# Local attention blocks: probabilities turned whole and placed by copies, the sum of the rotated keys on another engine

## The reference, cut to what matters

```python
def look(t):
    p = jnp.pad(t, ((0, 0), (0, 0), (1, 0), (0, 0), (0, 0)))
    return jnp.concatenate([p[:, :, :nw], p[:, :, 1:]], axis=3)
...
q = l2norm(q) * qs
k = l2norm(k) * ksc
...
k = k * cos * inv + rotate_half(k) * sin * inv
...
sim = jnp.einsum('bhwie,bhwje->bhwij', bq, bk2) * QK_SCALE
sim = jnp.where(mask, -jnp.finfo(sim.dtype).max, sim)
attn = jax.nn.softmax(sim, -1)
out = jnp.einsum('bhwij,bhwje->bhwie', attn, bv2)
...
for i in range(DEPTH):
    x = attn_layer(shift_tokens(x), Wqkv[i], q_scale[i], k_scale[i], Wo[i]) + x
    x = ffn_layer(shift_tokens(x), ln_g[i], ln_b[i], W1[i], b1[i], W2[i], b2[i]) + x
return x
```

## Time and profile before

| | |
|---|---|
| median of 3 runs | 3162.67 us |
| lowest and highest | 3152.88, 3163.48 us |
| the profiled execution's own time | 3146.83 us |
| its span, first to last instruction | 3144.8 us |
| mean granted TensorE clock | 0.954 of full speed |
| busy, share of the span | TensorE 88%, VectorE 78%, ScalarE 67%, GpSimd 43% |
| copies of `v_edge`, 128 KB each | 96 |

### The profile page before, as it was taken

How to read it: one execution, slowest core, us unless ns; L and a number is a source line. 1 busy time by engine, 2 the same in 40 slices (tenths; PEclk the granted TensorE clock), 3 DMA queues, 4 the chain that set the end, 5 groups by cost and what they waited for, 6 DMA issues and landing times. The chain is left out here.

```text
span 3144.8 us, 72108 instructions
## 1 busy us (share of the span) xinstructions
PE 2774.6 (88%) x27244; PEld 1692.0 (54%) x27244; DVE 2442.2 (78%) x3071; ACT 2104.3 (67%) x3079; POOL 1351.6 (43%) x1209
## 2 busy tenths in 40 slices
PE   5799999997678989888889898989999999789997
PEld 3122222223546565656566666656665656478885
DVE  3899999992379797979798888888888979455554
ACT  2488888885158787878788787878787878311111
POOL 1000000000078685867586758676766767200000
PEclk7799999998589999999999999999999999889998
DMA  3011111100010001000100010001000000000001
GB/s 131 27 29 28 28 29 29 29 24 8 8 57 9 6 9 43 7 8 9 42 9 6 17 34 9 8 15 36 8 7 14 15 7 9 12 18 0 0 0 34
DMA packets 56465, 64.35 MB, mean 20 GB/s; under 512 B 24742, under 2 KB 38964, under 8 KB 55348
## 3 DMA queue, kind: packets, MB, share of 16 engines
q1 hardware_dynamic: 55380, 60.58, 7.0%
q10 hardware_dynamic: 864, 0.79, 0.1%
HBM read 36.69 MB, written 7.34 MB: 14 GB/s over the span
## 5 line engine op out<-in xcount | busy, mean ns | idle before, releaser
L886 DVE TENSOR_REDUCE a_minus_max<-a_ps_max 128x1 f32<-128x1024 f32 x512 | 596.8, 1218 | 57.6 <-PE a_ps_max L811 52.3
L794 ACT ACTIVATE a_expT<-a_ps_scoresT 128x512 f32<-128x512 f32 (+1 forms) x683 | 528.8, 808 | 78.2 <-PE a_ps_scoresT L829 67.4
L1178 POOL TENSOR_TENSOR b_turned_q<-b_rot_q,b_turned_q 128x1024 f32<-128x1024 f32 x96 | 226.8, 2362 | 270.2 <-DVE b_turned_q L1549 257.3
L844 PE MATMUL a_ps_out<-a_expT,v_aug 128*32 128x256 f32 x4096 | 327.9, 392 | 5.4 <-ACT a_outT L781 4.8
L1620 DVE STREAM_TRANSPOSE b_probsT<-b_probs 32x512 f32<-32x512 f32 x384 | 269.4, 702 | 11.9 <-POOL b_probs L1219 0.3
L765 POOL CAST a_max_hi<-a_minus_max 128x16 bf16<-128x16 f32 x32 | 6.3, 198 | 631.1 <-DVE a_minus_max L886 631.1
L1287 ACT ACTIVATE b_kT<-b_psD 64x512 f32<-64x512 f32 x384 | 226.1, 589 | 58.6 <-PE b_psD L1374 53.5
L829 PE MATMUL a_ps_scoresT<-a_q_op,a_k_op 26*128 26x512 bf16 x1024 | 247.2, 385 | 13.1 <-ACT a_expT L794 4.4
L1225 POOL TENSOR_TENSOR b_turned_k<-b_rot_k,b_turned_k 128x512 f32<-128x512 f32 x192 | 243.9, 1270 | 0.2 <-DVE b_turned_k L1549 0.2
L1185 POOL TENSOR_TENSOR b_rot_q<-b_turned_q,b_inv_norm 128x1024 f32<-128x1024 f32 x96 | 182.8, 1904 | 137.7 <-issue 137.7
L1219 POOL TENSOR_TENSOR b_probs<-b_probs,b_inv_sum 128x512 f32<-128x512 f32 x192 | 197.3, 1049 | 99.1 <-DVE b_inv_sum L1593 99.1
(11 more groups left out here) (295 smaller groups left out, 6019.4 us busy)
## 6 DMA issues: line engine op xcount, KB each, us to landing
b_v_edge<-b_v SPq DMA_DIRECT2D x96, 128.0 KB
b_w_qkv<-L_ffn_Wqkv SPq DMA_DIRECT2D x6, 1536.0 KB
a_q_op<-terms_q SPq DMA_DIRECT2D x128, 48.0 KB
a_k_op<-terms_k SPq DMA_DIRECT2D x128, 48.0 KB
joined<-a_outT SPq DMA_DIRECT2D x256, 16.0 KB
b_w_o<-L_ffn_Wo SPq DMA_DIRECT2D x6, 512.0 KB
a_q_op<-a_max_rows SPq DMA_DIRECT2D x128, 4.0 KB
b_w<-L_ffn_W SPq DMA_DIRECT2D x6, 341.0 KB
```

The lines of the kernel that those rows point to most:

```text
L794: act.activation(expT[:, to:to + 512 * size], ps_scoresT[:, at:at + 512 * size], ACT.Exp, scale=SCALE_A).then_inc(exp_ready, 1)
L844: last_mm = pe.matmul(ps_out[lo:lo + 32, 256 * part:256 * part + 256], v_aug[:, b * T8 + kt, head, :], expT[:, at:at + 256], start=(kt == ...
L886: dve.tensor_reduce(minus_max[p % 2][:, side, 0, qt:qt + 1], ps_max[u % 2][:], AX.X, ALU.max, negate=True).then_inc(max_taken, 1)
L1178: pool.tensor_tensor(turned[:], rot[:], turned[:], ALU.add).then_inc(added, 1)
```

## The change

The own half of the probabilities is transposed in one instruction over all 128 partitions into a new buffer `packed_own`, as the look-back half was into `packed`. `probsT` is laid out as partition, window of the query, head, 32 queries, so that every block of 32 partitions and one window is one run of 512 numbers. From the two buffers eight copies issued by SP, each of 32 partitions by 512 numbers, place the blocks: four out of `packed` (one to `edgeT`, three to `probsT`) and four out of `packed_own`. The copies of ScalarE (L1272, L1273) and GpSimd (L1201) go, with `ones`. The value matmuls read their 128 columns as four pieces of 32.

The sum of the two key products is formed by VectorE, in one instruction over all 16 heads right behind the second product; GpSimd's two additions go, and its two multiplications wait for that sum.

The next layer's 1.5 MB of projection weights are loaded in six parts of 256 KB, one in each step of the loop of a layer's first half, behind the eight copies.

VectorE waits for the previous tile's copies to have left `packed` and `packed_own` before it writes them again; TensorE waits for all eight in front of the value matmuls.

```diff
-        probsT = sb("probsT", [P, HEADS_B, P])
+        packed_own = sb("packed_own", [P, HEADS_B, W])
+        probsT = sb("probsT", [P, P // W, HEADS_B, W])
         edgeT = sb("edgeT", [P, HEADS_B, W])
-        ones = sb("ones", [P, HEADS_B])
...
+            def load_qkv_part(l, slot, part):
+                at = slot * 3 * INNER + part * 512
+                sp.dma_start(w_qkv[:, ds(at, 512)], wts["Wqkv"][ds(l, 1), :, ds(part * 512, 512)].rearrange("o p n -> p (o n)")).then_inc(w_qkv_in, 16)
...
             def step(l, b, s, par, lags, ahead=None):
+                T = l * TILES + b * T8 + s
                 if 0 in lags:
-                    T = l * TILES + b * T8 + s
                     sp.wait_ge(v_held, 2 * T + 2)
                     sp.dma_start(v_edge[par][P - W:P, :], v[1 - par][P - W:P, :]).then_inc(v_edge_in, 16)
+                if 1 in lags:
+                    sp.wait_ge(packed_ready, T)
+                    if 2 in lags:
+                        sp.wait_ge(out_half, 2 * (T - 1))
+                    sp.dma_start(edgeT[P - W:P], packed[0:W]).then_inc(back_placed, 16)
+                    for j in range(1, P // W):
+                        sp.dma_start(probsT[W * j - W:W * j, j], packed[W * j:W * j + W]).then_inc(back_placed, 16)
+                    sp.wait_ge(packed_own_ready, T)
+                    for j in range(P // W):
+                        sp.dma_start(probsT[W * j:W * j + W, j], packed_own[W * j:W * j + W]).then_inc(own_placed, 16)
+                if b == 0 and not isinstance(s, int) and not (isinstance(l, int) and l == LAST):
+                    load_qkv_part(l + 1, (l + 1) % 2, s - 2)
...
                     load_scales(l + 1)
-                    load_qkv(l + 1, (l + 1) % 2)
...
-                    pool.wait_ge(out_half, 2 * (T - 2))
-                    pool.wait_ge(packed_ready, T - 1)
...
-                    for j in (2, 3):
-                        rows = slice(W * j, W * j + W)
-                        pool.tensor_tensor(probsT[W * j - W:W * j, :, rows], packed[rows], ones[rows].unsqueeze(2).to_broadcast([W, HEADS_B, W]),
-                                           ALU.mult).then_inc(high_back_ready, 1)
-                        pool.wait_ge(high_back_ready, 2 * (T - 2) + j - 1)
...
-                    pool.wait_ge(parts_k_ready, 2 * T + 2)
+                    pool.wait_ge(sum_k_ready, T + 1)
                     for half in range(2):
                         heads = slice(8 * half, 8 * half + 8)
-                        pool.tensor_tensor(turned_k[:, heads], rot_k[:, heads], turned_k[:, heads], ALU.add).then_inc(sum_k_ready, 1)
-                        pool.wait_ge(sum_k_ready, 2 * T + half + 1)
...
-                    act.activation(edgeT[P - W:P], packed[0:W], ACT.Copy).then_inc(low_back_ready, 1)
-                    act.activation(probsT[0:W, :, W:2 * W], packed[W:2 * W], ACT.Copy).then_inc(low_back_ready, 1)
...
-                    pe.wait_ge(probsT_ready, 4 * (T - 1))
-                    pe.wait_ge(low_back_ready, 2 * (T - 1))
-                    pe.wait_ge(high_back_ready, 2 * (T - 1))
+                    pe.wait_ge(own_placed, 64 * (T - 1))
+                    pe.wait_ge(back_placed, 64 * (T - 1))
...
-                                pe.matmul(psD[half][rows, at:at + P], v[par][:, DH * head:DH * head + DH], probsT[:, head, :],
+                                pe.matmul(psD[half][rows, at:at + P].rearrange("p (j w) -> p j w", w=W), v[par][:, DH * head:DH * head + DH], probsT[:, :, head, :],
                                           start=(pair % 4 == 0), stop=False, skip_group_check=True)
...
                     rotary_sin(psK, turned_k, parts_k_ready, 2)
+                    dve.wait_ge(parts_k_ready, 2 * T + 2)
+                    dve.tensor_tensor(turned_k[:], rot_k[:], turned_k[:], ALU.add).then_inc(sum_k_ready, 1)
...
                     if 2 in lags:
-                        dve.wait_ge(low_back_ready, 2 * (T - 1))
-                        dve.wait_ge(high_back_ready, 2 * (T - 1))
-                        dve.wait_ge(out_half, 2 * (T - 1))
+                        dve.wait_ge(back_placed, 64 * (T - 1))
                     dve.transpose(packed[:], probs[:, :, 0, :]).then_inc(packed_ready, 1)
...
-                    for j in range(P // W):
-                        rows = slice(W * j, W * j + W)
-                        dve.transpose(probsT[rows, :, rows], probs[rows, :, 1, :]).then_inc(probsT_ready, 1)
-                        if j == 0 and ahead:
-                            scale(ahead[0], ahead[1], 0)
+                    if 2 in lags:
+                        dve.wait_ge(own_placed, 64 * (T - 1))
+                    dve.transpose(packed_own[:], probs[:, :, 1, :]).then_inc(packed_own_ready, 1)
+                    if ahead:
+                        scale(ahead[0], ahead[1], 0)
```

More of the change, by code:

```diff
@@ L1007, in local_blocks @@
         packed_ready = sem("packed_ready")
-        probsT_ready = sem("probsT_ready")
-        low_back_ready = sem("low_back_ready")
-        high_back_ready = sem("high_back_ready")
+        packed_own_ready = sem("packed_own_ready")
+        back_placed = sem("back_placed")
+        own_placed = sem("own_placed")
         out_half = sem("out_half")
@@ L1139, in _ @@
             load_mlp(0)
+            sp.wait_ge(zeroed, 9)
             stream(sp, step, middle)
@@ L1148, in _ @@
             pool.memset(edgeT[:], 0.0).then_inc(zeroed, 1)
-            pool.memset(ones[:], 1.0).then_inc(zeroed, 1)
             for i in range(2):
                 pool.memset(v_edge[i][:], 0.0).then_inc(zeroed, 1)
-            pool.wait_ge(zeroed, 8)
+            pool.wait_ge(zeroed, 7)
             for b in range(BATCHES):
                 pool.memset(y[64:P, column(b * T8):column(b * T8) + 1], 0.0).then_inc(zeroed, 1)
-            pool.wait_ge(zeroed, 10)
+            pool.wait_ge(zeroed, 9)
             def tokens_of(t, par):
@@ L1239, in _ @@
         def _(act):
-            act.wait_ge(zeroed, 10)
+            act.wait_ge(zeroed, 9)
             def norm_start(l, b, n):
@@ L1267, in step @@
                         act.activation(qT[:, 4 * half:4 * half + 4, :].rearrange("p a b -> p (a b)"), psD[half][:], ACT.Copy).then_inc(qT_held, 1)
-                if 2 in lags:
-                    act.wait_ge(packed_ready, T - 1)
-                    act.wait_ge(out_half, 2 * (T - 2))
-                    act.activation(edgeT[P - W:P], packed[0:W], ACT.Copy).then_inc(low_back_ready, 1)
-                    act.activation(probsT[0:W, :, W:2 * W], packed[W:2 * W], ACT.Copy).then_inc(low_back_ready, 1)
                 if 0 in lags:
@@ L1337, in _ @@
         def _(pe):
-            pe.wait_ge(zeroed, 10)
+            pe.wait_ge(zeroed, 9)
             def mean(l, b, n, ended):
@@ L1363, in step @@
                 if isinstance(s, int) and s == 0 and b == 0 and 0 in lags:
-                    pe.wait_ge(w_qkv_in, 16 * (l + 1))
+                    pe.wait_ge(w_qkv_in, 16 + 16 * 6 * l)
                 w_at = l % 2 * 3 * INNER
@@ L1514, in _ @@
         def _(dve):
-            dve.wait_ge(zeroed, 10)
+            dve.wait_ge(zeroed, 9)
             def centre(l, b, n):
@@ L1572, in step @@
                     if 2 in lags:
-                        dve.wait_ge(probsT_ready, 4 * (T - 1))
+                        dve.wait_ge(packed_own_ready, T - 1)
                     rows = probs[:].rearrange("p h c k -> p h (c k)")
```

## The result

| | before | after |
|---|---|---|
| median of the runs | 3157.78 us (4 runs, 3144.27 to 3163.48) | 3249.31 us (4 runs, 3247.69 to 3262.1) |
| span of the profiled execution | 3144.8 us | 3246.0 us |
| mean granted TensorE clock | 0.954 | 0.945 |
| median interval without an MLP | 15.94 us | 16.60 us |
| mean interval with an MLP (11) | 40.7 us | 44.1 us |

A forecast was written before the change was run, and what follows sets the result against it. VectorE, full at 15.92 us per plain tile, and a TensorE-ScalarE-GpSimd circle nearly as long were taken to bind. 18 us gained over 84 plain intervals less 10 lost at 11 with an MLP gave 8: 3155 us, range 3108 to 3205.

The forecast's parts named there:

- Two circles of nearly one length: Plain tile: VectorE is full at 15.92 us, TensorE-ScalarE-GpSimd nearly as long; relieving one pays only until the other binds.
- the circle without GpSimd's wait: TensorE and ScalarE in a plain tile: ScalarE's 0.60 us wait goes, so 15.92 falls to 15.32 us.
- Transposes and reading in four pieces: Plain tile: one full transpose replaces four, saving VectorE 2.21 us; four-piece reading costs TensorE zero, at most 0.06 us.
- The addition: VectorE's key addition takes 1.25 us plus a delay of 0 to 0.97 beside GpSimd's probability multiplication; 0.97 was taken.
- Rival B: VectorE's addition is not delayed; the circle of TensorE and ScalarE binds at 15.32 us, time 3112; chance 0.32.
- VectorE's sum: VectorE's own period in a plain tile with the addition delayed: 15.55 to 15.93 us.
- The third circle: Value matmuls, exponential, row sum, addition, transpose, eight issues at 0.51, landing 1.8, value matmuls again: 15.6 us if delayed.
- Rival C: Copies land late, TensorE waits for the eighth: circle 12.1 + 7 x spacing; 3205 at 0.60, 3246 at 0.67; chance 0.18.
- The weights and the layer's start: SP's queue: six weight pieces fit behind the eighth copy; layer-start loads and scales, about 11.7 us, just covered by 11.8.

## Why the prediction was wrong

- **What bounds it, right.** Two circles of nearly one length: the copies alone free VectorE of 2.0 us a tile and win nothing, and 15.32 for the circle without GpSimd's wait was measured as 15.33.
- **Transposes and reading in four pieces, right.** The full transposes take 0.70 and 0.71 us, and sixteen value matmuls 1.09; copies alone ran at 0.9992.
- **The addition, right.** 1.25 + 0.97 = 2.22 was taken; 2.07 was measured, 1.32 where it meets only the end of GpSimd's multiplications and 1.18 where it meets none. The Trainium skill, "SBUF — State Buffer", section "Who interferes with whom", says that a VectorE instruction with two SBUF inputs contends with a GpSimd instruction that reads SBUF. These rows agree. L1578, from which the 0.97 was taken, reads a single tensor, so its row was not this case, and the rule as the prediction tells it does not explain it. Rival B falls.
- **VectorE's sum, too high.** 15.55 to 15.93 was taken; with the addition held up and no own copies the period was 15.33 to 15.40. It bound nothing in the changed kernel.
- **The third circle: its form right, its sizes wrong. This is the step that failed.** "I take 0.51" for the spacing, from `v_edge`, which goes alone; a row of eight measured 0.633, and the row of eight that I had, 0.67, was the nearer kind. Over the burst that is 4.35 - 7 x 0.51 = 0.78 us. The eighth copy then took 2.25 us from issue to matmuls, 2.01 to land and 0.24 until TensorE began, where 1.8 and 0.05 were allowed: 0.40 more. SP's own wake-up took 0.12 instead of 0.05. From the value matmuls to the end of the transpose into `packed` it was 9.92 us instead of 10.16, 0.15 of the difference by the addition. 15.63 + 0.78 + 0.40 + 0.07 - 0.24 = 16.64 us, the time between the value matmuls at 1286.52 and 1303.16 above; the median is 16.60. Rival C, at 0.18, is what happened; its own formula gives 12.1 + 7 x 0.633 = 16.53 for the period and (16.53 - 15.92) x 84 + 10 = 61 us lost. That its 3246, for a spacing of 0.67, lies next to the measured 3249 is luck: the spacing was smaller, and a third of the loss came another way.
- **What no case had.** The other 30 of the 91.5 us by which the medians differ, and how the loss is spread: the formula has 51 us in the plain intervals and 10 in those with an MLP; the trace has 36 less 10 in ordinary ones, 33 in nine long ones and 38 in those with an MLP. Late copies were priced as a wait of one length; the nine tiles in which a copy came a microsecond later still, with TensorE idle for over 2 us and then at a lower clock (0.50 to 0.67 over 3.2 us), were not foreseen. Nor was that the tiles in front of an MLP wait for copies as well: 10 us were taken for the 11 intervals, for the addition alone (0.9 each; 0.7 by the run with the addition alone, 1.2 by the one without own copies), and they lost 38.
- **The weights and the layer's start, right:** free, by the run with the weights in one piece and by the trace: in the second layer the scales are issued by 1239.2 us, and the first copies behind them go at 1246.7.

## What to carry to other kernels

A chain of copies is priced by its count times the spacing of issues that follow each other, read from a row of such issues, and not from a lone one; bytes did not matter here. When a wait is put into a loop of two nearly equal circles, ask first which instruction in front of it can be moved: the same parts, with one addition one place later, turned 3% of loss into 1.7% of gain. And a wait of TensorE can have a second price, its clock.

## What the hardware showed that was not expected

- A packet of the instruction queue (16 KB, 0.9 to 1.5 us of a DMA engine's time) coincides with nearly every late group of copies, 18 of 19, and with all 17 for which TensorE stood. That it is the cause was not tried by itself.
- In the changed kernel 13 of the 14 waits of 2.0 to 2.7 us in front of value matmuls were followed by a lower granted clock, 0.50 to 0.70 over 3.2 us, with sixteen value matmuls of up to 1.97 us instead of 1.09. Waits of 1.24 us in plain tiles left it at 1.00, and so did four of 1.6 to 1.7. The wait's length alone does not decide: with nine copies some waits of 2.0 to 2.9 us left it at 1.00.
- What TensorE's sequencer still has to do behind a landing counts: two instructions were 0.21 us between the landing and the matmuls, four 0.41.
